# Attention and feed-forward kernel on one core: the small operations that split a unit's maxima are placed one by one between the maxima, ScalarE rounds the projections' high part, and the jobs of the step table move

## The chip, the cores and the metric

The kernel runs on one core of one Trainium2 chip. The metric is the device time of one execution in microseconds (us). The engines are named as the profile names them: PE (TensorE, with PEld for its weight loads), DVE (VectorE), ACT (ScalarE), POOL (GpSimd) and SP (SyncE, which only issues DMAs here).

## The reference, cut to what matters

```
x = x + ga * attention(layernorm(x) * (1 + ca) + sa)      # 8 batches x 1024 tokens x 256, 16 heads of 16
x = x + gb * feed_forward(layernorm(x) * (1 + cb) + sb)   # two layers of windowed attention and a gated MLP

attention(h):
    inner, outer, v = h @ Wi, h @ Wo, h @ Wv              # per head: 1024 x 16
    p    = softmax(inner @ outer.T / 4)                   # over 1024 keys
    attn = p * aperture[q] * expression[k]
    attn = attn / (attn.sum(keys) + 1e-8)
    out  = (fixed per-head rotation and scale of attn @ v) @ Wout
```

The change touches the attention alone. Its softmax needs the maximum of every query's row of logits. The feed-forward part is the same code before and after.

## The kernel before, in words

**Two stages.** The attention works through eight batches, 64 steps each, and then the feed-forward part starts. Batch 0 and batch 7 are written out straight; batches 1 to 6 are one loop body.

**Units and steps.** A batch has eight units (`u`): a group of four heads times one half of the queries. A unit has eight steps, one for each 128 keys. In step `e` PE computes transposed logits for step `e+1` in two pairs of heads (`st`, line 655), ACT takes their exponentials (`exp`, line 938, two of 128x1024), and PE multiplies those of step `e` with the values (`pv`, line 667).

**Maxima.** The exponent of a query needs its row's maximum beforehand. So for each unit PE also computes the logits the other way round, 32 blocks of 128 queries by 512 keys (`score`, line 637), and DVE reduces each to a column of maxima (`maximum`, line 1153). Four scores and four maxima go with each step, and they run `AHEAD` = 48 blocks ahead of the unit that uses them. When a unit's 32nd maximum is there, DVE combines the halves and splits the result into three bf16 parts with five operations of 128x16 (`split`, lines 1161 to 1169), each waiting for the one before. PE transposes the parts (`maxima`, line 644), DVE copies them to `mrow` (`rows`, line 1174), and SP moves the rows by three small DMAs (line 436) into `stack`, where the `st` of that unit's first step (step 7 modulo 8 of the unit before it) reads them as an extra term. With 48 blocks ahead the split falls behind the last maximum of steps 3, 11, 19, ... (3 modulo 8), and the transposition and the copy fall into steps 4, 12, 20, ...

**Banks.** Banks 5 to 7 of PSUM form a ring. The scores and the jobs below take the next bank in the order of the list `ring`: in a step with a job that is score, job, score, score, score. A tenant waits on PE until the reader of the tenant three places before it is done (`bank_free`, `taken`). So in a step with a job the last score waits for the job's reader.

**Jobs.** The table `between` gives a step at most one job: `heads` (PE transposes a unit's result, DVE normalises it, steps 2 modulo 8), `maxima` (above), `cvT` and `out` (output projection of the previous batch; DVE adds the residual), and for the next batch `hT` (transposes of the normalised input), `proj` (eight blocks 128x512 of the two f32 projections, two f32 matmuls each, line 619) and `v`.

**The projections' split.** A projection block becomes three bf16 parts. DVE copies it to bf16 (line 1129, the high part, into one of four slots of `parts`), subtracts that from the block (line 1131, into `rest`), and POOL makes the middle and low parts (lines 1572 and 1575). SP writes the four slots out (line 408) and later reads them as stacks (line 427). A slot's high part may be written only when the slot's last write-out has landed (`s_parts_out`). In a `proj` step PE runs the first matmul of the block behind the first score and the second behind the third; DVE runs the copy and the subtraction behind its third maximum.

**Order on the engines.** Each engine's order is written out by hand, in the `batch` function of each block: PE (`early`, `late`), ACT, DVE, POOL, SP.

## Time and profile before

| | us |
|---|---|
| three runs | 5584.57, 5597.72, 5596.64 |
| median | 5596.64 |
| the profiled execution | 5589.1 |
| its span, first to last instruction | 5587.3 |
| PE busy in the span | 5159.0 (92%) |
| DVE busy | 4149.6 (74%) |
| ACT busy | 2768.1 (50%) |
| POOL busy | 1136.2 (20%) |

The span is what the trace shows; the time of the profiled execution is 1.8 us more, and the median of the runs is 7.5 us above that execution. Busy time is the union of an engine's instructions. "Idle" in a row is the time the engine stood still just before it, and behind the arrow stands what released it. The granted clock (PEclk) is 1.00 at 2.4 GHz and 0.50 at 1.2 GHz. Times inside the span count from its start. Batch 4, the fourth pass of the loop body, runs from 1165.2 us (the first maximum of its step 0) to 1421.1 us (the same of batch 5); most rows are from it, and where a step is timed it goes from its first maximum to that of the next step.

### The profile page before, as it was taken

Reading aid. Unit: us, or ns where it says so; the run is one execution under the profiler, and the core shown is the slowest. Engines: PE = TensorE matmul, PEld = TensorE weight load, DVE = VectorE, ACT = ScalarE, POOL = GpSimd, SP = SyncE. Lnnn points to the kernel's source line nnn. Section 1 sums busy time; section 2 is a strip of 40 time slices with the busy share of each in tenths; the row PEclk is TensorE's granted clock in tenths of the full one; section 3 lists DMA queues with packets and bytes.
Section 4 is the critical chain, followed back from the end, with each engine's and each line's share of the span. In section 5 each row is a group of like instructions: output and inputs, shape, how many; then the busy total and the mean of one; then the engine's idle time right before and its main releaser. Section 6 shows DMA issues by size and latency. Waiting matters only on the chain.

```text
span 5587.3 us, 93191 instructions
## 1 busy us (share of the span) xinstructions
PE 5159.0 (92%) x29772; PEld 3087.8 (55%) x29772; DVE 4149.6 (74%) x10975; ACT 2768.1 (50%) x5457; POOL 1136.2 (20%) x1469
## 2 busy tenths in 40 slices
PE   4899898999989997999999999999999999999998
PEld 1233333333333334777776777777767777777776
DVE  4787777787777784777777777776777777777776
ACT  0555555555555564444444444444444544445444
POOL 2202021111112001222222222222222222222221
PEclk7999999999999999999999999999999999999999
DMA  4422233322233221000000000000000000000000
GB/s 108 105 48 56 40 62 45 63 50 46 51 54 61 39 39 33 11 7 7 9 8 28 7 11 7 6 11 28 7 11 6 7 9 26 11 9 8 7 8 6
DMA packets 165077, 160.91 MB, mean 29 GB/s; under 512 B 26228, under 2 KB 157128, under 8 KB 164560
## 3 DMA queue, kind: packets, MB, share of 16 engines
q1 hardware_dynamic: 164688, 156.42, 13.2%
q8 instruction: 159, 2.61, 0.2%
q14 instruction: 230, 1.88, 0.1%
HBM read 111.48 MB, written 44.09 MB: 28 GB/s over the span
## 4 chain that ended last, share of the span: by engine, by line
PE 73%; DVE 16%; issue 6%; SPq 1%; POOL 1%; DMA 1%; ACT 0%; DVEq 0%; POOLq 0%; ACTq 0%
PE psum L875 13%; PE psum L807 9%; PE psum L637 8%; PE psum L667 7%; PE psum L655 6%; PE psum L782 6%; DVE mx L1153 5%; PE psum L846 4%; PE psum L855 4%; PE psum L838 4%; PE psum L830 3%; PE psum L819 2%; DVE big_s L1349 2%; DVE big_s L1364 1%; PE psum L627 1%
## 5 line engine op out<-in xcount | busy, mean ns | idle before, releaser
L1153 DVE TENSOR_REDUCE mx<-psum 128x1 f32<-128x512 f32 x2048 | 1322.6, 687 | 405.8 <-PE psum L637 395.6
L938 ACT ACTIVATE pr<-psum 128x1024 f32<-128x1024 f32 x1024 | 1021.2, 1023 | 868.4 <-PE psum L655 860.4
L637 PE MATMUL psum<-stack 96*128 96x512 bf16 x2048 | 748.7, 396 | 170.2 <-DVE mx L1153 101.9
L995 ACT ACTIVATE big_s<-big_s,mxl_s 128x256 f32<-128x256 f32 x1024 | 507.5, 496 | 654.3 <-DVE mxl_s L1357 654.3
L875 PE MATMUL psum<-hlT_s,w_sb 128*128 128x128 f32 (+1 forms) x6144 | 786.5, 281 | 24.3 <-DVE hlT_s L1394 22.0
L875 PEld LDWEIGHTS psum<-hlT_s,w_sb 128*128 128x128 f32 (+1 forms) x6144 | 692.5, 179 | 158.0 <-ACT hlT_s L1010 55.3
L807 PE MATMUL psum<-wqkv_sb,uT_s 128*128 128x512 f32 x1536 | 747.8, 610 | 1.0 <-DVE uT_s L1310 1.0
L637 PEld LDWEIGHTS psum<-stack 96*128 96x128 bf16 x2048 | 199.4, 97 | 886.3 <-DVE mx L1153 381.7
L655 PE MATMUL psum<-stack 99*128 99x512 bf16 x2048 | 627.9, 389 | 31.4 <-issue 25.7
L667 PE MATMUL psum<-pr,vg 128*32 128x512 f32 x4096 | 564.6, 624 | 0.4 <-ACT pr L938 0.4
L830 PE MATMUL psum<-kT_s,qz_s 128*128 128x256 f32 x2048 | 516.8, 391 | 0.0
L1349 DVE CUSTOM_DVE_ANT_0 big_s<-psum,mask_s,rn_s 128x256 f32<-128x256 f32 x1024 | 437.5, 478 | 12.0 <-PE psum L830 5.4
L830 PEld LDWEIGHTS psum<-kT_s,qz_s 128*128 128x128 f32 x2048 | 367.1, 192 | 112.6 <-ACT qz_s L987 52.2
L1623 POOL TENSOR_TENSOR rn_s<-ss_s,neghalf 128x8 f32<-128x8 f32 x256 | 420.2, 1656 | 19.3 <-POOL ss_s L1619 0.5
L977 ACT ACTIVATE pT_s<-psum 128x1024 f32<-128x1024 f32 x128 | 131.1, 1024 | 566.8 <-PE psum L807 565.3
L782 PE MATMUL psum<-w_sb,pT_s 128*128 128x256 f32 (+1 forms) x1536 | 393.4, 398 | 6.9 <-issue 5.1
L807 PEld LDWEIGHTS psum<-wqkv_sb,uT_s 128*128 128x128 f32 x1536 | 264.7, 192 | 230.0 <-issue 198.3
L782 PEld LDWEIGHTS psum<-w_sb,pT_s 128*128 128x128 f32 (+1 forms) x1536 | 272.8, 190 | 102.3 <-issue 60.0
L1364 DVE TENSOR_SCALAR big_s<-big_s,rz_s 128x256 f32<-128x256 f32 x1024 | 315.7, 351 | 18.2
L655 PEld LDWEIGHTS psum<-stack 99*128 99x128 bf16 x2048 | 202.4, 100 | 214.8 <-issue 75.1
L1405 DVE SCALAR_TENSOR_TENSOR pT_s<-psum,b_sb,pT_s 128x128 f32<-128x128 f32 (+1 forms) x768 | 209.0, 343 | 122.7 <-ACT pT_s L1018 115.2
L1018 ACT ACTIVATE pT_s<-psum,b_sb 128x128 f32<-128x128 f32 (+1 forms) x768 | 216.5, 367 | 167.2 <-PE psum L875 166.4
(165 smaller groups left out, 6565.1 us busy)
## 6 DMA issues: line engine op xcount, KB each, us to landing
stack<-parts_d SPq DMA_DIRECT2D x384, 128.0 KB, 5.8
parts_d<-parts SPq DMA_DIRECT2D x64, 384.0 KB, 2.6
hn<-in_x SPq DMA_DIRECT2D x8, 1024.0 KB, 8.1
xr<-in_x SPq DMA_DIRECT2D x8, 1024.0 KB, 5.5
x_d<-xr SPq DMA_DIRECT2D x8, 1024.0 KB, 8.7
tab<-tab_d SPq DMA_DIRECT2D x32, 256.0 KB, 2.6
mask_s<-in_mask SPq DMA_DIRECT2D x64, 128.0 KB, 2.2
out_x<-o_s SPq DMA_DIRECT2D x64, 128.0 KB, 1.7
```

Source lines behind the costliest of these rows:

```text
L637: pe.matmul(psum[:, to, :], stack[0:KS, g % 2, 0, u % 2, h, a * P:(a + 1) * P], stack[0:KS, g % 2, 1, kh, h, :], start=True, stop=True).th ...
L655: mm = pe.matmul(psum[:, h, :], stack[0:KS + PART, (u // 2) % 2, 1, kc // 4, h, (kc % 4) * P:(kc % 4 + 1) * P], stack[0:KS + PART, (u // 2 ...
L667: mm = pe.matmul(psum[h * VW:(h + 1) * VW, ACC, :], vg[:, (u // 2) % 2, kc, h, :], pr[:, e % 2, h, :], start=(kc == 0), stop=(kc == NT - 1))
L782: mm = pe.matmul(psum[:, bk, 0:D], hid[0:rows, cc, :], w2_sb[0:rows, l, cc, :], start=(cc == 0), stop=(cc == FC - 1))
L807: mm = pe.matmul(psum[:, bk + m, :], w["uT"][:, l, k * (P + 1):k * (P + 1) + P], wqkv_sb[:, l, k, m * INNER:(m + 1) * INNER], start=(k == ...
L830: mm = pe.matmul(psum[:, bk + h // 2, (h % 2) * 2 * P:(h % 2 + 1) * 2 * P], w["qz"][:, h, :], w["kT"][:, l, h // 2, :], start=True, stop=True)
L875: mm = pe.matmul(psum[0:rows, bk + 1 + m // 4, (m % 4) * P:(m % 4 + 1) * P], w1_sb[:, l, k, col:col + rows], w["hlT"][:, k, :], start=(k = ...
L938: act.activation(pr[:, e % 2, 2 * pair:2 * pair + 2, :], psum[:, 2 * pair:2 * pair + 2, :], ACT.Exp, scale=DH ** -0.5).then_inc(s_exp, 1)
L995: ins = act.activation(w["big"][:, h, :], w["big"][:, h, :], ACT.Exp, bias=w["mx"][:, h:h + 1], accum_out=w["z"][:, h:h + 1])
L1153: dve.tensor_reduce(mx[:, u % 2, m, kh:kh + 1], psum[:, src, :], AX.X, ALU.max).then_inc(s_max, 1)
L1349: ins = dve.tensor_tensor_reduce(out=w["big"][:, h, :], in0=psum[:, bk + h // 2, (h % 2) * 2 * P:(h % 2 + 1) * 2 * P], in1=w["mask"][:], s ...
L1623: gp.tensor_tensor(w["rn"][:, half_h], w["ss"][:, half_h], neghalf[:, 0:LH], ALU.pow).then_inc(w["s_rn"], 1)
```

## The change

1. The five operations of `split` are taken apart. The first stands behind the second maximum of the following unit, and the other four behind the next four maxima, one each.
2. `AHEAD` goes from 48 to 51. A unit's last maximum is now the first of step 3 modulo 8; the five operations stand in steps 3 and 4 modulo 8 (two, then three), and the `maxima` job moves from steps 4 to steps 5 modulo 8, in PE's order from behind the third score to behind the first, in DVE's (`rows`) from behind the third maximum to behind the second.
3. ACT writes a projection block's high part (`high_part`), between the two exponentials of the step; it waits for PE and for the slot. DVE waits for ACT (`s_hi`) and only subtracts, now behind its second maximum.
4. Both matmuls of a projection block run together behind the first score.
5. The jobs are placed anew around the `maxima` steps.

```
-AHEAD = MU + 16
+AHEAD = MU + 19
...
-            between[NT * u + 4] = ("maxima", u + 1)
-        for kind, places in (("cvT", (5, 6, 7, 8)), ("out", (9, 11, 13, 15)), ("hT", (23, 24, 25, 27)),
-                             ("proj", (29, 31, 33, 35, 37, 39, 41, 43)), ("v", (38, 40, 45, 46, 47, 48, 49, 51))):
+            between[NT * u + 5] = ("maxima", u + 1)
+        for kind, places in (("cvT", (4, 6, 7, 8)), ("out", (9, 11, 12, 14)), ("hT", (22, 23, 24, 25)),
+                             ("proj", (28, 30, 31, 33, 35, 36, 38, 40)), ("v", (39, 41, 43, 44, 46, 47, 48, 49))):
...
+            def high_part(b, n, src):
+
+                act.wait_ge(s_proj, b * BLOCKS + (n + 1))
+                act.wait_ge(s_parts_out[n % 4], FREE + b * 32 + 16 * (n // 4))
+                act.activation(parts[:, n % 4, 0], psum[:, src, :], ACT.Copy).then_inc(s_hi, 1)
...
             def split_block(b, n, src, prev):
 
-                c0, ps = b * (2 * BLOCKS), psum[:, src, :]
-                dve.wait_ge(s_proj, b * BLOCKS + (n + 1))
-                dve.wait_ge(s_parts_out[n % 4], FREE + b * 32 + 16 * (n // 4))
+                dve.wait_ge(s_hi, b * BLOCKS + (n + 1))
                 if prev or n >= 2:
-                    dve.wait_ge(s_part, c0 + (2 * n - 2))
-                dve.tensor_copy(parts[:, n % 4, 0], ps).then_inc(s_rest, 1)
-                dve.wait_ge(s_rest, c0 + (2 * n + 1))
-                dve.tensor_tensor(rest[:, n % 2], ps, parts[:, n % 4, 0], ALU.subtract).then_inc(s_rest, 1)
+                    dve.wait_ge(s_part, b * (2 * BLOCKS) + (2 * n - 2))
+                dve.tensor_tensor(rest[:, n % 2], psum[:, src, :], parts[:, n % 4, 0], ALU.subtract).then_inc(s_rest, 1)
...
                 def next_maximum(q):
                     if not absent("score", q, first, last):
                         maximum(b, q, bank(place["score", q]))
+                    u, step = (q - MU) // MU, (q - MU) % MU - 1
+                    if 0 <= step < 5 and not absent("maxima", u, first, last):
+                        split(b, u, step)
...
                     next_maximum(q0 + 1)
+                    if kind == "proj":
+                        split_block(b + 1, n, src, True)
+                    elif kind == "maxima":
+                        rows(b, n, src)
                     next_maximum(q0 + 2)
-                    if kind == "maxima":
-                        rows(b, n, src)
-                    elif kind == "proj":
-                        split_block(b + 1, n, src, True)
-                    elif kind == "out":
+                    if kind == "out":
                         residual(b, n, src)
                     elif kind == "v":
                         logits(b + 1, n, src)
                     next_maximum(q0 + 3)
-                    if (q0 + 3) % MU == MU - 1 and not absent("score", q0 + 3, first, last):
-                        split(b, (q0 + 3) // MU)
```

**What moves on DVE around a unit's split.** The place is in batch 0, steps 18 to 20; the first row starts behind the normalisation of step 18, `m` and `mr` are the split, `mrow` the copied rows. Before:

```order
L1153 TENSOR_REDUCE mx<-psum 128x1 x7
L1161 TENSOR_TENSOR m<-mx 128x16
L1163 CAST m<-m 128x16
L1165 TENSOR_TENSOR mr<-m 128x16
L1167 CAST m<-mr 128x16
L1169 TENSOR_TENSOR m<-mr,m 128x16
L1153 TENSOR_REDUCE mx<-psum 128x1 x3
L1174 COPY mrow<-psum 48x128
```

The same place of the changed kernel, steps 18 to 21:

```order
L1158 TENSOR_REDUCE mx<-psum 128x1 x6
L1167 TENSOR_TENSOR m<-mx 128x16
L1158 TENSOR_REDUCE mx<-psum 128x1
L1170 CAST m<-m 128x16
L1158 TENSOR_REDUCE mx<-psum 128x1
L1173 TENSOR_TENSOR mr<-m 128x16
L1158 TENSOR_REDUCE mx<-psum 128x1
L1176 CAST m<-mr 128x16
L1158 TENSOR_REDUCE mx<-psum 128x1
L1179 TENSOR_TENSOR m<-mr,m 128x16
L1158 TENSOR_REDUCE mx<-psum 128x1 x3
L1184 COPY mrow<-psum 48x128
```

The count of operations is the same; one reduction stands between any two of the five, and the rows' copy comes a step later.

**What moves on PE in a projection step.** The place is in batch 0, the first block of batch 1 (`hT,wi_sb`) with the scores (`stack`, line 637), the transposed logits (line 655) and the product with the values (`pr,vg`). Before:

```order
L637 MATMUL psum<-stack 128x512
L619 MATMUL psum<-hT,wi_sb 128x512
L655 MATMUL psum<-stack 128x512 x2
L637 MATMUL psum<-stack 128x512 x2
L619 MATMUL psum<-hT,wi_sb 128x512
L667 MATMUL psum<-pr,vg 32x512 x4
L637 MATMUL psum<-stack 128x512
```

and of the changed kernel:

```order
L638 MATMUL psum<-stack 128x512
L621 MATMUL psum<-hT,wi_sb 128x512 x2
L656 MATMUL psum<-stack 128x512 x2
L638 MATMUL psum<-stack 128x512 x2
L668 MATMUL psum<-pr,vg 32x512 x4
L638 MATMUL psum<-stack 128x512
```

The second matmul of the block has moved ahead of the transposed logits and of two scores.

## Rows read from the trace of the kernel before

**Rows 1.** The page: busy time by engine.
```profile
PE 5159.0 (92%) x29772; PEld 3087.8 (55%) x29772; DVE 4149.6 (74%) x10975; ACT 2768.1 (50%) x5457; POOL 1136.2 (20%) x1469
```

**Rows 2.** Windows: batches 0, 4 and 7; stretch, length, busy times, PEclk, DMA.
```profile
147.40:392.50 245.10, 219.09 (x1141) 73.25 (x1140) 195.56 (x376) 136.53 (x150) 40.43 (x36) 0.98 0.31 68
1165.20:1421.10 255.90, 230.76 (x1193) 83.47 (x1192) 199.22 (x383) 138.99 (x153) 40.79 (x37) 0.96 0.28 52
1929.10:2103.40 174.30, 164.40 (x912) 55.80 (x911) 147.12 (x277) 107.27 (x114) 4.08 (x7) 1.00 0.24 38
```

**Rows 3.** Windows: batch 4, steps 32; 18 to 21; 51 to 53; 9 to 15.
```profile
1284.11:1286.95 2.84, 2.84 (x17) 1.04 (x16) 2.60 (x5) 1.86 (x3) 2.11 (x3) 1.00 1.14 128
1233.88:1247.14 13.26, 12.12 (x70) 3.84 (x69) 11.94 (x27) 7.84 (x9) 0.00 (x0) 1.00 0.58 165
1373.41:1384.90 11.49, 9.73 (x54) 3.19 (x53) 8.88 (x20) 6.45 (x9) 0.00 (x0) 1.00 0.02 3
1199.01:1228.20 29.19, 27.41 (x148) 11.77 (x146) 23.79 (x53) 14.16 (x16) 19.74 (x12) 1.00 0.20 29
```

**Rows 4.** Windows: batch 4, steps 31; 40; 43; 36 and 37; 44 and 45.
```profile
1278.85:1284.11 5.26, 4.62 (x21) 1.49 (x20) 3.92 (x7) 2.72 (x4) 0.85 (x2) 1.00 1.15 143
1323.20:1327.35 4.15, 3.88 (x21) 1.67 (x20) 2.73 (x6) 2.35 (x4) 0.92 (x1) 1.00 0.27 95
1336.21:1343.01 6.80, 5.08 (x23) 1.59 (x21) 5.44 (x12) 3.42 (x4) 1.76 (x2) 1.00 0.00 2
1302.45:1313.80 11.35, 9.91 (x35) 3.26 (x36) 6.77 (x12) 2.29 (x4) 0.85 (x2) 0.71 0.11 37
1343.01:1353.39 10.38, 9.36 (x35) 3.57 (x36) 5.53 (x12) 2.67 (x5) 0.00 (x0) 0.67 0.11 39
```

**Rows 5.** Timeline, steps 18 to 21: start, length, engine, line, operation, [idle before <- releaser].
```profile
1235.52 4.51 DVE L1153 TENSOR_REDUCE mx<-psum 128x1 f32<-128x512 f32 x7
...
1240.06 0.17 DVE L1161 TENSOR_TENSOR m<-mx 128x16 f32<-128x16 f32 x1
...
1241.00 1.89 DVE L1153 TENSOR_REDUCE mx<-psum 128x1 f32<-128x512 f32 x3
1241.74 0.39 PE L637 MATMUL psum<-stack 96*128 96x512 bf16 x1 [1.14 <-DVE mx L1153]
...
1242.80 0.21 DVE L1174 COPY mrow<-psum 48x128 bf16<-48x128 bf16 x1
1243.09 1.84 SPq L436 DMA_DIRECT2D stack<-mrow  x3
```

**Rows 6.** Timeline, batch 5, step 3: a small operation that waits for none before it.
```profile
1437.20 0.17 DVE L1169 TENSOR_TENSOR m<-mr,m 128x16 bf16<-128x16 f32 x1
1437.29 0.22 DVE L1148 TENSOR_SCALAR za<-zt 128x128 f32<-128x128 f32 x1
```

**Rows 7.** Timeline, step 31: a projection step on PE, DVE and ACT.
```profile
1280.37 1.29 DVE L1153 TENSOR_REDUCE mx<-psum 128x1 f32<-128x512 f32 x2 [0.82 <-PE psum L637]
1280.38 1.02 PE L619 MATMUL psum<-hT,wi_sb 128*128 128x512 f32 x2
...
1281.57 0.68 DVE L1129 CAST parts<-psum 128x512 bf16<-128x512 f32 x1
1282.29 0.69 DVE L1131 TENSOR_TENSOR rest<-psum,parts 128x512 f32<-128x512 f32 x1
1282.55 0.60 ACT L932 ACTIVATE o_sb<-psum 128x512 f32<-128x512 f32 x1 [1.38 <-PE psum L667]
...
1283.04 0.39 PE L637 MATMUL psum<-stack 96*128 96x512 bf16 x1 [0.64 <-DVE rest L1131]
...
1283.46 2.60 DVE L1153 TENSOR_REDUCE mx<-psum 128x1 f32<-128x512 f32 x4 [0.48 <-PE psum L637]
```

**Rows 8.** Timeline, the queue of SP: the first write-outs of slots in batch 4.
```profile
1291.33 10.77 SPq L408 DMA_DIRECT2D parts_d<-parts  x4
```

**Rows 9.** Landing of the rows' DMAs (line 436) in batch 4.
```profile
DMA to landing us min/median/max: 1.6/1.8/2.7
```

65 lines of the change are left out of this document (37 added, 28 removed).

## The prediction

> **What bounds the kernel now.** I read the page's busy times first: PE is busy 92% of the span, DVE 74%, ACT 50% [rows 1]. That is a mean over two stages, and only the attention is touched, so the windows come next, batch by batch and then step by step. Batch 4 takes 255.9 us and PE is idle in 25.1 of them, with a mean granted clock of 0.96 [rows 2]. A step without a job takes 2.84 us, with PE busy for all of it and DVE for 2.60 [rows 3]. So a plain step is bound by PE, with DVE only 0.24 behind, and anything on DVE beyond that shows up as PE waiting for a bank of the ring. Two places do so. The timeline of steps 18 to 21 shows the split: PE's only idle time in 13.26 us is 1.14 us, in front of a score that waits for the maximum behind the five small operations [rows 3, 5]. The projection steps take 5.26 us with PE busy for 4.62, and end in a score that waits 0.64 us for DVE's subtraction [rows 4, 7]. Where both meet the step takes 6.80 us, and the 10.38 us right behind it (steps 44 and 45) run at a granted clock of 0.67, the 11.35 us of steps 36 and 37 at 0.71 [rows 4], which is a mix of the levels 2.4 and 1.2 GHz after PE has stood still.
>
> **The change, part by part.** I cost it for a full batch, in batch 4's rows.
>
> *Split, in a unit with light steps.* DVE runs seven reductions back to back from 1235.52 to 1240.06, 0.65 us each from start to start although each is listed with 0.69, then the five operations up to 1241.00, 0.94 us, each waiting for the one before [rows 5]. In the new order two of the five stand before that reduction, apart from each other, and need not wait. What such an operation costs DVE no row shows for the split itself. The nearest is the `za` operation, which starts 0.09 us after a small operation it doesn't depend on [rows 6]; the other end is the whole 0.17 us, or 0.94/5 = 0.19. I take 0.09, since the reductions' 0.65 against 0.69 shows the same overlap. The reduction at 1241.00 then starts at 1240.24, and the score at 1241.74 is 0.76 us earlier. Some 0.1 of it is lost again: the other three operations and the row copy add 0.4 us to DVE where it has 0.24 a step to spare. Gain 0.65 us; the ends are 0.3 (at 0.19 each) and 1.14 (no idle time left). The step with the transposition gives back nothing more, since PE and DVE do the same work there as before.
>
> Here the Trainium skill speaks against the change. VectorE: DVE Perf Modes, section "The DRAIN you can't avoid", says that the next operation doesn't start until the pipeline has emptied, with or without semaphores between, and advises to cut the number of operations, which this change leaves as it is. The trace disagrees in part: 0.09 from start to start for an operation 0.17 long [rows 6]. By that rule the gain would be the lower end, some 22 us less in the whole.
>
> *Split, beside jobs.* What the split and the transposition cost now above the bare steps: steps 43 and 44, 6.80 - 5.26 = 1.54 and about 0.47 for the transposition's step, together 2.0, and the same for 35 and 36; steps 51 to 53, 11.49 against 4.15 + 2 x 2.84, is 1.66 [rows 3, 4]; for the units of steps 11 and 27 I take the 1.3 of the light unit (13.26 against 3.44 for a step with heads and 3 x 2.84; 3.44 is my reading of step 18). In the new table the steps beside jobs (11 and 12, 28, 35 and 36, 43 and 44) have DVE idle before the second maximum, so only what stands between the second maximum and the job's reader counts: 0.1 to 0.2 a step and 0.2 for the transposition, 0.5 a unit. Saved: three light units 2.0, unit 11 0.7, unit 27 0.8, units 35 and 43 3.0, unit 51 (light from now on) 1.0. **7.5 us.** Steps 9 to 15, 29.19 us now [rows 3], should take 28.4.
>
> *Projection steps.* Now the last score stands 2.66 us behind the start of the second matmul: 1.19 to the copy, 0.72 to the subtraction, 0.69 for it, 0.06 to PE [rows 7]. In the new order the second matmul starts 0.87 earlier, as four bf16 matmuls of some 0.22 no longer stand before it (my estimate: a step of 2.84 has eight of them beside the values' product). From there PE needs 0.9 for the matmul and 0.65 up to the second score, whose reduction starts 0.42 behind it [rows 7]; that reduction ends 2.4 behind the matmul's start. ACT has the high part by 1.19 + 0.60 = 1.8 (priced like its other 128x512 copy [rows 7]), so DVE doesn't wait for ACT; the subtraction ends at 3.05 and the score follows at 3.05. The step gains 0.87 + 2.66 - 3.05 = 0.48. PE's own work sets the floor at 4.6, a gain of 0.65; if ACT's copy came late the gain could go to nothing. ACT's copy itself is hidden: ACT is busy for 2.72 of 5.26 us [rows 4]. Its cover would be gone only if the second exponential came later than the next step's product, some 2 us on. Eight steps: **3.9 us.**
>
> *Clock.* Steps 36 and 37 take 11.35 against about 3.3 + 5.26, steps 44 and 45 10.38 against 3.3 + 4.15 [rows 4]: 2.8 and 2.9 us, both right behind a step of 6.80. With those steps at about 5 us and PE's idle time there cut to some 0.3, I expect the clock to stay at 2.4 GHz. **5.7 us.** The ends are nothing and this. Batch 0 shows 0.98 where batch 4 shows 0.96 [rows 2], so I give it none.
>
> *Waits that move.* ACT now waits for the slot of block 4, with the exponentials queued behind it. The write-outs start at 1291.33, 12.5 us behind the start of step 31 [rows 4, 8]. Blocks 4 to 7 are needed from step 35 on, 4.8 + 2.8 + 4.8 + 3.4 = 15.8 us behind the start of step 31, and the trigger in step 30 comes 1.9 earlier relative to it, as that step grows; so the slot should be free with over 2 us left. The rows of maxima go out 2.6 us later (from 1.8 us behind the start of step 20 to 4.4), while step 23 comes 0.65 earlier. They leave at 1243.09 in three issues of 0.6 us and land 1.8 us later [rows 5, 9], at 1246.1, and are needed at about 1249.6, so 3.5 us of cover shrink to 0.2. That is nothing at the median landing and 0.7 at the longest, 2.7 [rows 9], in the units with light steps behind.
>
> *Start and end.* Three more scores stand before batch 0 (1.9 us), three fewer in batch 7 (0.8 back). **1 us lost.** The first projection blocks are paced by POOL's two operations and the DMAs; nothing.
>
> *Sum.* Full batch: 7.5 + 3.9 + 5.7 = 17.1, six times 103. Batch 0 has 11.4. Batch 7 has no jobs for a next batch, seven units at 0.65: 4.5. 103 + 11 + 4.5 - 1 = 117 or 118. From the profiled execution's 5589.1 that gives 5472. The median of the runs stands 7.5 above that execution, so I put the median at **5475 us**, 2.2% less.
>
> **The rivals.**
> *A, small operations don't overlap.* Each costs DVE 0.19 wherever it stands. For it: the 0.94 for five. Against: 0.09 for `za` [rows 5, 6]. About 0.35 less a unit over 62 units is 22 us: 5497.
> *B, the clock falls all the same*, behind other idle times (the projection steps keep some). For it: it falls twice in batch 4 for reasons of which I know only that idle time went before. Against: step 31 has 0.64 idle and shows 1.00 [rows 4, 7]. 5.7 x 6 = 34 us: 5509.
> *C, slower: the maxima's rows land too late.* The first `st` of each unit waits for three DMAs, and PE's whole queue stands behind it. It has 0.2 us left. The 62 units save 1.9 each, so it decides from a landing of some 3.9 us instead of 1.8. If the rows came behind a large load and took 6 us, each unit would wait 4.0, 248 us against 117: 5605 to 5610. Against it: 2.7 was the longest of 24 [rows 9].
> *D, no change*: C in part, or ACT waiting for slots, eats what is gained: 5590.
>
> **How the numbers follow.** The forecast has 0.64, A 0.14, B 0.13, D 0.04, C 0.05. The forecast's own range runs from all idle time of the units gone (62 x 0.5 = 30 us) and the projections at PE's floor (9 us), 5436, to the lower ends of both, about 5495. With A and B the range is **5436 to 5515**, which leaves out C and D and little else. A measurement of this kernel can tell some 0.3%, 17 us, from no change. Faster by more than that: forecast, A, B, and a little of D, 0.92; within 0.3% 0.04; slower 0.04.
>
> **What would show it.** In the changed profile: steps 18 to 21 in about 12.6 us with 0.5 us of PE idle; a small operation between two reductions moving the next one by about 0.1; projection steps at 4.8 us, the score behind the subtraction waiting some 0.2; steps 35 to 37 and 43 to 45 at a clock of 1.00, full batches at 0.98 and near 239 us. It is wrong if steps 7 modulo 8 begin with PE waiting for the rows' DMAs, if ACT is idle before a high part in steps 35 to 40, or if low-clock stretches appear inside a batch.

## The result, and the profile after

The changed kernel takes 5416.08 us (median of 4 runs, 5414.40 to 5417.96), the kernel before 5590.60 (5583.30 to 5597.72) beside it: a ratio of 0.9688, with an interval of 0.9671 to 0.9705. That is 3.1% less. The prediction said 5475 and a range of 5436 to 5515: the sign was right, and the gain, 175 us of span (5587.3 to 5412.5), is half as much again as the 118 forecast. The time lies 20 us below the lower end of the range.

The busy line of the page, changed kernel, which answers to [rows 1]:
```profile
PE 5115.0 (95%) x29772; PEld 3075.7 (57%) x29772; DVE 4064.5 (75%) x10911; ACT 2800.6 (52%) x5521; POOL 1135.6 (21%) x1469
```
DVE has 64 instructions less and ACT 64 more, the high parts. PE's instructions are as many as before; of what went, 131 us are its idle time (428 us before and 298 now) and 44 us its busy time, which is shorter where the clock is no longer low.

Windows of the changed kernel: batches 0 and 4, which answer to [rows 2]; batch 7 up to the feed-forward stage; the feed-forward stage.
```profile
147.92:377.23 229.31, 217.21 (x1141) 72.50 (x1140) 184.94 (x368) 140.53 (x158) 40.36 (x36) 0.98 0.33 70
1081.03:1316.19 235.16, 225.58 (x1193) 81.71 (x1192) 188.43 (x376) 143.17 (x162) 40.76 (x37) 0.99 0.31 57
1779.04:2023.10 244.06, 211.79 (x1134) 75.92 (x1133) 159.58 (x314) 134.80 (x146) 16.15 (x24) 0.94 0.21 45
2023.10:5412.50 3389.40, 3269.78 (x20197) 2413.95 (x20195) 2527.33 (x7852) 1649.47 (x4221) 797.09 (x1144) 1.00 0.03 10
```
The last two of these in the kernel before:
```profile
1929.10:2179.70 250.60, 211.11 (x1136) 75.83 (x1135) 163.98 (x316) 134.50 (x146) 16.09 (x24) 0.95 0.22 44
2179.70:5587.30 3407.60, 3275.25 (x20198) 2414.13 (x20196) 2527.89 (x7852) 1649.05 (x4221) 797.45 (x1144) 0.99 0.03 10
```
Batch 4 takes 20.7 us less, batch 0 15.8, batch 7 6.5 between these borders. The fourth window is the surprise: the feed-forward stage, whose code the change doesn't touch, is 18.2 us shorter.

Windows inside batch 4 of the changed kernel: steps 18 to 21; 51 to 53; 9 to 15; 31; 36 and 37; 44 and 45 ([rows 3, 4] before).
```profile
1146.73:1159.02 12.29, 12.26 (x71) 3.88 (x70) 11.59 (x27) 7.85 (x9) 0.00 (x0) 1.00 0.76 192
1272.83:1281.49 8.66, 8.66 (x50) 2.48 (x48) 8.17 (x20) 5.96 (x8) 0.00 (x0) 1.00 0.01 2
1113.26:1141.05 27.79, 27.43 (x147) 11.75 (x146) 23.14 (x53) 14.15 (x16) 18.36 (x12) 1.00 0.18 25
1191.19:1195.99 4.80, 4.63 (x21) 1.49 (x20) 3.12 (x7) 3.21 (x5) 1.99 (x3) 1.00 1.08 147
1212.66:1219.97 7.31, 7.05 (x36) 2.17 (x35) 6.16 (x15) 3.62 (x6) 1.82 (x3) 1.00 0.01 3
1245.39:1252.81 7.42, 6.99 (x38) 2.54 (x37) 5.72 (x16) 4.34 (x6) 0.00 (x0) 1.00 0.01 2
```
Read the first number behind the stretch, its length, against the second, PE's busy time: in the light steps PE is now busy for all but 0.03 us. Steps 18 to 21 take 12.29 in batch 4 but 12.09 or 12.10 in four of the six batches of the loop, where the kernel before takes 13.27 in each. Steps 51 to 53 held a `v` job in the kernel before and hold none now, so their two rows are not of the same work. The projection step is at 4.80, as forecast, and the two places behind the old 6.80 us steps run at a clock of 1.00.

Timeline of DVE in steps 19 and 20 of batch 4, changed kernel, which answers to [rows 5]:
```profile
1152.39 0.69 DVE L1158 TENSOR_REDUCE mx<-psum 128x1 f32<-128x512 f32 x1 [0.16 <-PE psum L638]
1153.00 0.16 DVE L1170 CAST m<-m 128x16 bf16<-128x16 f32 x1
1153.07 0.68 DVE L1158 TENSOR_REDUCE mx<-psum 128x1 f32<-128x512 f32 x1
1153.67 0.16 DVE L1173 TENSOR_TENSOR mr<-m 128x16 f32<-128x16 f32 x1
1153.76 0.68 DVE L1158 TENSOR_REDUCE mx<-psum 128x1 f32<-128x512 f32 x1
```
From one reduction's start to the next it is 0.68 or 0.69 us with a small operation between them, 0.65 without [rows 5]. So a single operation listed with 0.16 costs 0.03 to 0.04 there.

**Where the 174.8 us went**, with batch starts taken at the first reduction of step 0: the feed-forward stage 18.2; batch 0 15.8; batches 1 to 6 134.7 (1536.6 to 1401.9), batch 7 6.6, less 0.5 for the start. Of the 134.7, 13.7 lie at the five places where the loop over the batches goes back (steps 63, 0 and 1: 16.9 to 21.2 us each before, 14.9 to 16.9 now; e6_before_pad217 below has the attention's code of the kernel before and its five edges took 6.0 less than those of the kernel before, so the 13.7 is good to some 6 us); the other 121 are 20.2 a batch, where 17.1 were forecast.

### The profile page after: what moved, and what is told of

Same layout as the page of the kernel before. It is cut to its first block, busy times and chain, and to the rows that moved or that the text cites. A ratio compares the mean times of both kernels' runs of the same rounds, so it can differ in the third digit from the quotient of the medians.

```text
span 5412.5 us, 93107 instructions
## 1 busy us (share of the span) xinstructions
PE 5115.0 (95%) x29772; PEld 3075.7 (57%) x29772; DVE 4064.5 (75%) x10911; ACT 2800.6 (52%) x5521; POOL 1135.6 (21%) x1469
## 4 chain that ended last, share of the span: by engine, by line
PE 77%; DVE 12%; issue 5%; SPq 2%; DMA 2%; POOL 1%; ACT 0%; DVEq 0%; POOLq 0%; ACTq 0%
PE psum L874 14%; PE psum L806 10%; PE psum L638 8%; PE psum L656 7%; PE psum L668 7%; PE psum L781 7%; PE psum L845 5%; PE psum L854 4%; PE psum L829 4%; PE psum L837 4%; DVE mx L1158 3%; PE psum L818 2%; PE psum L621 2%; DVE big_s L1361 2%; DVE big_s L1376 1%
## 5 line engine op out<-in xcount | busy, mean ns | idle before, releaser
L638 PE MATMUL psum<-stack 96*128 96x512 bf16 x2048 | 732.3, 391 | 56.4 <-DVE zt L1142 16.8
L668 PE MATMUL psum<-pr,vg 128*32 128x512 f32 x4096 | 550.3, 610 | 0.4 <-ACT pr L943 0.4
L1376 DVE TENSOR_SCALAR big_s<-big_s,rz_s 128x256 f32<-128x256 f32 x1024 | 315.5, 350 | 18.2
```

The lines of the kernel that those rows point to most:

```text
L638: pe.matmul(psum[:, to, :], stack[0:KS, g % 2, 0, u % 2, h, a * P:(a + 1) * P], stack[0:KS, g % 2, 1, kh, h, :], start=True, stop=True).th ...
L668: mm = pe.matmul(psum[h * VW:(h + 1) * VW, ACC, :], vg[:, (u // 2) % 2, kc, h, :], pr[:, e % 2, h, :], start=(kc == 0), stop=(kc == NT - 1))
```

## The experiments

The theory to be tested first is the prediction's: the gain within a batch is the split's idle time, the second matmul with ACT's copy, and the low clock. Rivals are named in the expectations. Each ran timed beside the kernel before. Batch lengths below are sums over the 64 steps of the median in batches 1 to 6: 256.7 us before, 234.4 changed.

**The two parts alone.** e1_split_only is the changed kernel with the projection as before:
```
-    act.activation(parts[:, n % 4, 0], psum[:, src, :], ACT.Copy)     # high_part
+    dve.tensor_copy(parts[:, n % 4, 0], ps)                           # split_block, behind the third maximum
     second matmul back in late()
```


> The changed kernel with the projections as they were before: DVE makes the high part and subtracts, both behind its third maximum, and PE runs a block's second matmul behind the third score. AHEAD, the table and the five separate operations stay as changed. Theory 1 (the split is most of the gain, the projections about 0.48 us for each of 8 blocks in 7 batches): 27 us over the changed kernel's 5416, so 5443 us, with light units still at 12.3 us, projection steps at 5.26, and no low clock inside a batch. Theory 2 (the projections' new form is what keeps PE going and the clock up): low clock back in steps 35 to 45 and 5480 us or more. Either may be off by some 18 us if the feed-forward loops come out in another state.

e2_proj_only is the kernel before with the changed projection, and the old tables, AHEAD and split.

> The kernel before with the projections alone in their new form: both matmuls behind the first score, ACT makes the high part, DVE subtracts behind its second maximum. AHEAD 48, the five chained operations and the old table stay. Theory 1: 8 x 0.48 us in 7 batches, 27 us off 5590, so 5563 us; the light units stay at 13.3 us, and since steps 35 and 43 still hold the split the clock still falls behind them. Theory 2: the falls of the clock go with the projections' waits, another 34 us, 5530 us.

Measured: 5477.47 us (0.9808, interval 0.9788 to 0.9827) and 5523.65 (0.9887, 0.9868 to 0.9906). Neither hit its number: e1 is 34 us above its 5443 and e2 6 below even its second theory. The reason lies outside the work of the two parts. The feed-forward stage is 3406.4 in e1 and 3393.8 in e2, and the five edges of the batch loop sum to 96.3 us in e1 and 79.2 in e2, against 93.8 before and 80.1 changed: both go with the projection part, which shortens DVE's code. Take them off, and e1 is 28 us above the changed kernel, where theory 1 had 27.

A batch takes 241.5 and 249.1, so 15.2 and 7.6 less than before, 22.8 together, near the 22.3 that both bring. That holds the edges. Inside the batches (means of steps 2 to 62) it is 239.1 before, 218.9 changed, 222.5 in e1 and 232.9 in e2: 16.6 and 6.2 less, 22.8 against 20.2. So the parts add up but for 2.6 us a batch. Each may remove a share of the same low clock; that isn't shown. The low clock is gone inside e1's batches although its projection steps still take 5.26, and stays in e2, whose steps 35 and 43 take 6.33.

**Are the small operations better apart?** e3_grouped:
```
-    if 0 <= step < 5 and not absent("maxima", u, first, last):
-        split(b, u, step)
+    if step == 0 and not absent("maxima", u, first, last):
+        for k in range(5): split(b, u, k)
```


> The changed kernel with one edit: the five small operations stand together again, chained, behind the second maximum of the next unit, where the first of them stands in the changed kernel. Theory 1 (what counts is that a maximum stands between any two): the chain costs DVE 0.94 us at once instead of some 0.3 in five places, PE idles about 0.7 us again in each of 62 units, so 5416 + 43 = 5459 us, light units at 13.0 to 13.3. Theory 2 (what counts is the new place, three blocks further ahead and away from the jobs, and the transposition a step later): under 10 us more, 5425.

e8_maxima_late puts the transposition behind the third score and the row copy behind the third maximum; e16_grouped_late does both; e9_ahead48 is e8 with `AHEAD = MU + 16`.

> The changed kernel, with the maxima's transposition back behind the third score of its step and the row copy back behind the third maximum (before the change they stood there too; the step stays the fifth of the unit, the five small operations stay apart, the projection as in the change). The kernel with the five operations together in the new place lost only 25 us of what the split part brings (85), so the place must bring most. Theory R (what counts is that transposition and row copy stand early in their step, beside the second score): per unit 0.5 to 0.8 us back, 62 units, 5450 to 5466, with a light unit (steps 18 to 21) at 12.9. Rival S (what counts is that the transposition comes a step later, so that PE has a full ring of scores ahead of it): within 8 us of the changed kernel, 5416 to 5424, light unit 12.3 to 12.4.

> The kernel with the late transposition (5429.9), and beside it AHEAD back at MU + 16: three scores fewer stand ahead. A unit's last maximum is then the fourth of its fourth step again, as before the change, and the five small operations follow behind the second to fourth maximum of the fifth step and the first two... of the sixth, apart from each other; the jobs stay at the changed steps. Theory S2 (what brings most of the split part's gain is that the chain of small operations begins just ahead of PE's values' product, which needs no bank, and the transposition comes with more scores ahead): per unit 0.3 to 0.7 us more than the late transposition, 5450 to 5475. Rival R2 (the gain is in having the operations apart and the transposition a step later, wherever the last maximum stands): 5425 to 5435.

> The changed kernel with both: the five small operations together behind the maximum after a unit's last one, and the transposition and row copy late in their step. Of the unit's three steps 19 to 21 the changed kernel takes 8.66 us, with the operations together 9.00, with the late transposition 8.83, the kernel before 9.83. If the two add up, 9.2 and 5416 + 25 + 14 = 5455; what is left to the kernel before, 0.65 a unit, is then the place of the last maximum and of the group in the step alone. If they don't (one stall covers the other), 9.0 and 5441.

Measured: e3 5441.25 (0.9740, 0.9721 to 0.9759), e8 5429.88 (0.9726, 0.9709 to 0.9744), e16 5451.57 (0.9770, 0.9753 to 0.9786), e9 5477.50 (0.9802, 0.9782 to 0.9823). Steps 59 to 61 of batch 4 have no job beside the split's; one window of each, in the order before, changed, e3, e8, e16, e9:
```profile
1400.03:1409.86 9.83, 8.69 (x50) 2.56 (x48) 8.62 (x20) 5.65 (x7) 0.00 (x0) 1.00 0.01 3
```
```profile
1296.61:1305.27 8.66, 8.66 (x50) 2.48 (x48) 8.17 (x20) 5.66 (x7) 0.00 (x0) 1.00 0.01 2
```
```profile
1312.99:1322.00 9.01, 8.84 (x50) 2.48 (x48) 8.47 (x20) 5.66 (x7) 0.00 (x0) 1.00 0.01 2
```
```profile
1305.62:1314.44 8.82, 8.69 (x50) 2.56 (x48) 8.13 (x19) 5.65 (x7) 0.00 (x0) 1.00 0.01 2
```
```profile
1313.75:1322.92 9.17, 8.86 (x50) 2.56 (x48) 8.43 (x19) 5.65 (x7) 0.00 (x0) 1.00 0.01 2
```
```profile
1332.04:1341.40 9.36, 8.74 (x50) 2.56 (x48) 8.14 (x20) 5.65 (x7) 0.00 (x0) 1.00 0.01 2
```
e3 leaves only 25 us to the operations' being apart, between its theories (5459 and 5425). The unit's gain of 1.17 us comes apart: keeping the operations together costs 0.35, the late transposition 0.16, both 0.51, so they add up. The other 0.66 is left to the place: the last maximum of a unit is now the first of its step and not the fourth. It isn't the transposition's coming a step later: its step takes 3.31 in e16 as in the kernel before. What differs is the step of the operations and one plain step, 3.68 + 2.84 before against 3.32 + 2.54 in e16. The timelines show what the place does. Before, the block of five begins at 1240.06, 1.1 us behind the end of PE's values' product, with the next product still to come; PE, three banks ahead at most, runs dry [rows 5]:
```profile
1237.91 1.07 PE L667 MATMUL psum<-pr,vg 128*32 128x512 f32 x8
```
In e3 the same block begins at 1167.38, just behind a product, where DVE has caught up:
```profile
1166.19 1.06 PE L668 MATMUL psum<-pr,vg 128*32 128x512 f32 x8
...
1169.05 0.39 PE L638 MATMUL psum<-stack 96*128 96x512 bf16 x1 [0.17 <-DVE mx L1158]
```
```profile
1167.38 0.16 DVE L1167 TENSOR_TENSOR m<-mx 128x16 f32<-128x16 f32 x1
...
1168.30 3.84 DVE L1158 TENSOR_REDUCE mx<-psum 128x1 f32<-128x512 f32 x6
```
It holds DVE as long as before (0.92 us), and the waiting score loses 0.17 in place of 1.14. e9 points the same way (0.54 more than e8; 5477.50 lies just above its 5475), but there the chain also ends later, which makes its transposition's step 3.81 where 3.31 stand in e8, so it isn't a clean measure of the place. e8 fits neither of its two theories: 0.16 a unit lies between 0 and 0.5, nearer to rival S. e16 is near its 5455.

**What a small operation costs.** e11_ten_small puts one more behind each of the five:
```
+    dve.tensor_copy(idle[:, 16 * step:16 * step + 16], ident[:, 0:16])
```


> The changed kernel, with one more small operation behind each of the five (a copy of 128x16, depending on nothing). It measures what a small operation costs VectorE where PE sets the pace. My reading of the trace of after (0.65 us from one reduction to the next, 0.68 with a small operation between): 0.07 to 0.1 each, 62 units of 5: 20 to 30 us if VectorE were the bound and 0 to 15 where it isn't; 5416 to 5432, and a light unit (steps 18 to 21) at 12.3 to 12.5. Rival A (each operation empties the pipeline, 0.19 or more each): 5 x 0.19 = 0.95 a unit against the spare time of 0.24 a step, 0.5 a unit longer, 5445 or more. The 39 places of code in the feed-forward stage may change too: its own length is read apart (3389 or 3407).

Measured: 5425.96 (0.9710, 0.9690 to 0.9730), and steps 59 to 61:
```profile
1300.55:1309.34 8.79, 8.79 (x50) 2.48 (x48) 8.40 (x24) 5.66 (x7) 0.00 (x0) 1.00 0.01 3
```
The unit pays 0.13 us for five. That isn't what they cost DVE, which has time to spare there. DVE's timeline in step 20 of batch 4 has that:
```profile
1156.40 0.68 DVE L1159 TENSOR_REDUCE mx<-psum 128x1 f32<-128x512 f32 x1
1157.00 0.17 DVE L1174 TENSOR_TENSOR mr<-m 128x16 f32<-128x16 f32 x1
1157.08 0.17 DVE L1222 COPY idle<-ident 128x16 f32<-128x16 f32 x1
1157.16 0.69 DVE L1159 TENSOR_REDUCE mx<-psum 128x1 f32<-128x512 f32 x1
```
From reduction to reduction it is 0.76 us with two small operations, 0.68 with one, 0.65 with none: the first costs 0.03, the second 0.08, as the expectation had it. Rival A of the prediction (0.19 each) has fallen: the unit would have to be 0.5 longer. Some 7 us of the time are not the unit's: the feed-forward stage is 3396 us, from another place of the code (below).

**What ACT brings.** e10_dve_high is the changed kernel, with DVE making the high part directly ahead of the subtraction; both matmuls stay early. e18_dve_high_front20 is the same with a filler in the set-up, explained below.
```
-    dve.wait_ge(s_hi, b * BLOCKS + (n + 1))
+    dve.tensor_copy(parts[:, n % 4, 0], ps).then_inc(s_rest, 1)
```


> The changed kernel, but VectorE makes the projection's high part again (copy, then subtraction, both behind the second maximum), with both matmuls in one piece early in the step as in the change. Theory A (ACT's taking the copy over is what brings the projection part's gain): VectorE has 0.69 us more in each of 8 steps of a batch, of which it has no spare time in those steps, so 8 x 0.65 = 5.2 us a full batch over the changed kernel's, more where it stands beside a split and the clock falls again; with the longer code before the feed-forward loops (39 instructions) that stage goes back to 3407: 5416 + 36 + 18 = 5470, up to 5490 with the clock. Rival E (the early second matmul brings it): 5435 to 5445.

> The kernel in which VectorE makes the high part (5493), with 20 such copies in the set-up: the attention loop starts 17 behind a block's start in place of 3 before it. Theory F: the second wait for code at the 5 loop edges goes, 97 us for the 5 in place of some 81 to 83: 14 to 16 us less, 5478; the feed-forward stage at 3407 as it was. What then lies between it and the changed kernel, 62 us, is 18 of the feed-forward stage and 44 of ACT's taking the copy (8 x 0.72 us in each of 7 batches is 40). Rival H (the edge is longer because VectorE itself is more loaded there): 5493.

Measured: 5493.22 (0.9831, 0.9812 to 0.9850) and 5476.26 (0.9793, 0.9778 to 0.9808). Step 31 of batch 4, e10:
```profile
1231.48:1237.00 5.52, 4.62 (x21) 1.49 (x20) 3.80 (x8) 2.72 (x4) 2.67 (x4) 1.00 1.15 129
```
5.52 against 4.80: ACT's part is 0.72 a step, a whole copy, 8 x 7 x 0.72 = 40 us. And 5.52 is longer than the 5.26 of the kernel before [rows 4] and of e1, from which e10 differs in two things: the second matmul is early, and DVE's copy and subtraction stand behind its second maximum. Together they cost 0.26 without ACT. So the early matmul is worth nothing by itself here. ACT's copy with the matmul left late was not run. e10 as a whole is 3 us above the 5490 that was its upper end; the 17.0 us that e18 takes less say what was missed, the edges of the batch loop.

**Does a stand-still of PE bring the low clock?** e15_stall:
```
+    if e in (35, 43) and not last:
+        for k in range(4): dve.tensor_reduce(idle[:, k:k + 1], wfold, AX.X, ALU.max)
```


> The changed kernel, with four reductions of 128x512 from SBUF added on VectorE behind the third maximum of steps 35 and 43 in all but the last batch (some 2.5 us each time, which PE must wait for as the ring has three banks). Theory C (a stand-still of PE there brings the low clock, which costs a few us more than itself): low-clock stretches inside the batch, in steps 36 and 44, some 2.5 us + 2 to 3 us each time, 14 places, 5416 + 63 to 77 = 5480 to 5493. Rival N (the low clock came of something else): each place costs 2.0 to 2.5 us and no low clock appears: 5444 to 5451.

Measured: 5450.11 (0.9770, 0.9754 to 0.9786). Steps 35 and 36 of batches 2 and 3 in e15:
```profile
744.07:755.26 11.19, 9.39 (x42) 3.16 (x41) 9.65 (x20) 5.07 (x7) 2.78 (x4) 1.00 0.16 56
982.68:995.31 12.63, 10.83 (x41) 3.14 (x39) 9.82 (x20) 5.08 (x7) 3.53 (x4) 0.86 0.12 41
```
The changed kernel takes 9.67 there. PE idles 1.80 us in both windows; in one the clock stays, in the other it falls, and that costs 1.44 more. It fell in 3 of the 14 places, all behind step 35 and none behind step 43. In time the rival is right (5450 in its 5444 to 5451), and theory C missed by 30 us or more; but three falls where the changed kernel has none say that a stand-still can bring one.

The added stand-still isn't the old one. PE's longest pause in one piece is 1.83 us at the end of steps 35 and 43 of the kernel before, with one of 0.64 ahead of it: the clock fell behind 11 of these 12 steps in batches 1 to 6. In e2 it is 1.83 with 0.17 ahead: 9 of 12. In e15 it is 1.63 in step 35 (3 of 7) and 1.56 in step 43 (none of 7), and in steps 11 and 51 of the kernel before some 1.5 (5 of 12). In e1's step 35 it is 0.72 and in the changed kernel 0.17 and 0.35: never. So longer pauses went with more falls, but the same pause in the same step gave both, and what decides was not found.

**The feed-forward stage.** The window loop of this stage exists twice in the code. Counted in DVE's compiled code, the change leaves 39 instructions less ahead of both copies, which begin at 1902 and 2885 in place of 1941 and 2924. e4_nops39 was to put 39 back as empty instructions; none of them was emitted, so it is a repeat of the changed kernel, and tells only how well that repeats.

> The changed kernel with 39 empty instructions on DVE between the attention and the feed-forward part, where DVE idles for 15 us on a DMA. They move DVE's later code by about as many instructions as the kernel before had more. Theory P (the feed-forward stage differs by 18 us between the two kernels only by where the code of DVE's two copies of the window loop lies, since the branch back takes 2.8 us in one state and 0.3 in the other): the first copy slow and the second fast again, about 18 us more, 5434 us, the attention unchanged. Rival (the feed-forward stage differs for another reason, as its start relative to the clock or to the DMAs): within 3 us of 5416.

It took 5418.18 (0.9697, 0.9678 to 0.9716). Real ones followed, copies of one column, where DVE waits for a DMA ahead of the stage (e5, e6, e7), or between the two copies (e12):
```
+    for j in range(39): dve.tensor_copy(idle[:, j:j + 1], ident[:, 0:1])     # e5; 217 in e6, 20 in e7, 40 in e12
```


> The changed kernel with 39 copies of one column more on VectorE, between the attention's last residual and the feed-forward stage, where VectorE waits some 15 us for a DMA. They move the two copies of VectorE's feed-forward window loop 39 instructions further, to the very places they have in the kernel before (loop starts at instructions 1941 and 2924 of VectorE's code in place of 1902 and 2885); the attention's code stays where it is. Theory P (the feed-forward stage became 18 us shorter only because shorter code before it put the loops at other places): VectorE's step back to the start of the loop takes 2.8 us in the first copy and 0.3 in the second, as before, the stage takes 3407 us in place of 3389, the whole 5434. Rival Q (the stage is shorter for another reason, such as the state in which the attention leaves the clock or the queues): 3389 and 5416 to 5420.

> The kernel before with 217 such copies at the same place: its loops start at 2158 and 3141, which is 256 instructions behind where the changed kernel has them. Theory P, with places that count modulo 256: first copy fast (0.3 us back), second slow (2.8), feed-forward stage 3389 to 3394, the whole 5572 to 5576, against 5588 of the kernel before; the 217 copies take some 13 us of VectorE, most of it in its 15 us of waiting. Rival Q: 3407 and 5588 or more. If places count over a longer period than 256 the state may be another one.

> The changed kernel with 20 such copies: loops start at 1922 and 2905, 130 and 89 modulo 256. Fast places so far are 108 and 110, slow ones 69 and 149. If the fast places form one stretch that reaches from 89 to 130, both copies are fast: 5 iterations of the second copy save 1.4 us each, stage 3382 to 3385, the whole 5409. If the stretch is narrow, both are slow: stage 3414, the whole 5441. One of each gives 3389 or 3407.

> The changed kernel with 40 copies of one column on VectorE between the first and the second copy of its feed-forward window loop (once in the run, 2 to 3 us of VectorE). The first copy stays at 1902 (110 modulo 256, fast), the second moves from 2885 to 2925 (69 to 109 modulo 256, where the fast ones have stood). Theory P: both copies fast, 5 x 1.4 = 7 us saved, less the 2 to 3 that the copies take: feed-forward stage 3384 to 3386, the whole 5411 to 5413. Rival Q2 (the second copy is slow for another reason than its place): 3392 and 5419.

Measured: e5 5435.81 (0.9741, 0.9725 to 0.9757), its stage 3410.0; e6 5570.28 (0.9979, 0.9969 to 0.9989), 3397.6; e7 5423.98 (0.9719, 0.9703 to 0.9736), 3396.3; e12 5413.31 (0.9684, 0.9664 to 0.9703), 3387.1. The timeline of DVE where the first copy of the loop steps back, kernel before:
```profile
2470.76 0.17 DVE L1357 TENSOR_SCALAR mxl_s<-mxl_s 128x4 f32<-128x4 f32 x1
2473.89 0.42 DVE L1285 TENSOR_TENSOR u_s<-psum,u_s 128x256 f32<-128x256 f32 x1 [2.96 <-issue]
...
2579.80 0.42 DVE L1285 TENSOR_TENSOR u_s<-psum,u_s 128x256 f32<-128x256 f32 x1 [2.93 <-issue]
```
Changed kernel:
```profile
2313.49 0.17 DVE L1369 TENSOR_SCALAR mxl_s<-mxl_s 128x4 f32<-128x4 f32 x1
2314.98 0.42 DVE L1297 TENSOR_TENSOR u_s<-psum,u_s 128x256 f32<-128x256 f32 x1 [1.33 <-PE psum L781]
...
2419.53 0.42 DVE L1297 TENSOR_TENSOR u_s<-psum,u_s 128x256 f32<-128x256 f32 x1 [1.32 <-PE psum L781]
```
And e5, the changed kernel with its code moved back to the old places:
```profile
2532.76 0.42 DVE L1300 TENSOR_TENSOR u_s<-psum,u_s 128x256 f32<-128x256 f32 x1 [2.96 <-issue]
```
Before, DVE waits 2.96 us at the step back for nothing that the profile shows; now it waits 1.33 for PE, as the loop's work wants. An iteration takes 105.9 in the one case and 104.55 in the other. Before, the first copy (15 steps back in all) pays and the second (5) doesn't; in the changed kernel it is the other way round: (15 - 5) x 1.36 = 14 us, and the rest of the 18 is the scatter of this stage, 3389 to 3397 in kernels with one code layout. e5 brings the wait and the 18 to 20 us back with nothing else changed, which settles it. e6 does the reverse in the kernel before, 256 places further than the changed kernel's loops, with a stage 10 us shorter. Both of e12's copies are free, and its 5413.31 is what was expected. e7's second copy, at 89 modulo 256, paid 2.8 us, against the first expectation; its first, at 130, was free.

**The loop over the batches.** It steps back across more code than any other, and each time DVE and ACT stand still for about 6 us (from the branch to the next instruction 4.8 to 6.8 us on DVE and 4.6 to 6.7 on ACT in the 20 traces). Some kernels show a second wait right behind. e13_before_front20 and e14_front30 have 20 and 30 of the one-column copies in the set-up, ahead of all loops, e17_front34 34.

> The kernel before with 20 copies of one column on VectorE in the set-up, where it waits 20 us. They move VectorE's attention loop from instruction 600 to 620 of its code (88 to 108 modulo 256), its feed-forward loops from 1941 and 2924 to 1961 and 2944. Theory F (after the step back VectorE comes to a second block of code some 5 to 8 instructions behind the loop's start, at about 96 modulo 256, and waits 3 to 5 us for it once more; in the changed kernel, which starts at 586, 22 instructions lie before it and it has come by then): with the start behind that point the second wait is gone, steps 63 to 1 of a loop edge take 15 to 17 us in place of 17 to 21, 6 edges 12 to 18 us in all, and the low clock there is shorter. The feed-forward copies: 169 modulo 256 slow as before, 128 fast as before, 3407. The whole 5570 to 5576 against 5588. Rival H (the edges are shorter because the changed jobs leave another backlog): 5588.

> The changed kernel with 30 such copies in the set-up, 29 instructions more in all: attention loop from 586 to 615 (103 modulo 256), feed-forward loops to 1931 and 2914 (139 and 98 modulo 256). If fast places are those from about 96 to 146 modulo 256, both feed-forward copies are fast, which saves 7 us and costs nothing elsewhere: stage 3382 to 3388. The attention's edges as they are, 15 to 17 us, or 0.5 us shorter each. The whole 5406 to 5411: the candidate that beats the changed kernel. If 98 lies before the boundary the second copy stays slow, 5416; if 139 is too late the first is slow, 5434.

> The changed kernel with 34 copies of one column on VectorE in the set-up (33 instructions more), where it waits 20 us. Its attention loop then starts at 13 of a block, its feed-forward loops at 46 and 2. Theory P: both copies at 104.6 us an iteration, no wait of 2.8 us at their steps back: stage 3382 to 3385, the whole 5408 to 5411, 0.13% less than the changed kernel. If 46 is too far (52 is slow) the first copy costs 15 x 1.4: 5430; if 2 is too near the start, the second copy costs 1.4 or 4.5 each time: 5416 or 5434.

Timeline of DVE behind the step back into a batch, kernel before:
```profile
1165.21 0.69 DVE L1153 TENSOR_REDUCE mx<-psum 128x1 f32<-128x512 f32 x1 [5.55 <-PE psum L637]
1166.49 0.69 DVE L1153 TENSOR_REDUCE mx<-psum 128x1 f32<-128x512 f32 x1 [0.59 <-PE psum L637]
1169.97 4.43 DVE L1153 TENSOR_REDUCE mx<-psum 128x1 f32<-128x512 f32 x7 [2.79 <-PE psum L637]
```
e10:
```profile
1116.83 0.69 DVE L1158 TENSOR_REDUCE mx<-psum 128x1 f32<-128x512 f32 x1 [5.88 <-PE psum L638]
1122.45 3.68 DVE L1158 TENSOR_REDUCE mx<-psum 128x1 f32<-128x512 f32 x6 [4.93 <-issue]
```
e18, the same kernel 20 instructions on:
```profile
1348.97 0.69 DVE L1159 TENSOR_REDUCE mx<-psum 128x1 f32<-128x512 f32 x1 [5.39 <-PE psum L639]
1350.25 1.29 DVE L1159 TENSOR_REDUCE mx<-psum 128x1 f32<-128x512 f32 x2 [0.59 <-PE psum L639]
1352.74 2.59 DVE L1159 TENSOR_REDUCE mx<-psum 128x1 f32<-128x512 f32 x4 [1.21 <-PE psum L639]
```
In e10 DVE does one reduction and waits 4.93 us once more; in the kernel before it does two, and the seven reductions that then run in one piece (1169.97) show that PE had the scores ready long before, so the 2.79 put down to PE are not PE's. In the compiled code both stand at the same instruction, 606, at which they stop: their loops begin at 603 and 600. The changed kernel's begins at 586, and by the time DVE gets there nothing is waited for. e18 takes 17.0 us less than e10; e13 took 5569.54 beside 5579.23 (0.9979, 0.9970 to 0.9989), its five edges 15.9 to 16.8 us in place of 16.9 to 21.2, 12 us in all.

e14 took 5434.47 (0.9737, 0.9721 to 0.9754), a miss: the second copy, at 98 modulo 256, pays twice. Its step back:
```profile
4859.73 0.42 DVE L1300 TENSOR_TENSOR u_s<-psum,u_s 128x256 f32<-128x256 f32 x1 [5.13 <-issue]
```
There DVE stops at the loop's start (2.8 us) and again two instructions on, at instruction 2916. Leaving out the labels, which are no instructions, 606 and 2916 are 576 and 2880: 2304 apart, 9 x 256. So both stops are at the starts of blocks of 256 instructions. Counted from a block's start (one more than in the later expectations, which had it one too far), the window loop of 333 instructions began, over all 20 kernels, at 3, 9, 10, 14, 29, 30, 34, 43, 47 and 129 where the step back took 0.3 us, and at 53, 73, 85, 226, 242, 246 and 255 where it took 2.8 or more. The Trainium skill, Runtime: NRT & Kernel Launch, section "Instruction fetch mechanics", says that an engine holds two pages of 256 instructions and that a step back to a page it no longer holds must fetch it first. The traces agree in kind, with 2.8 us for the window loop and about 6 for the batch loop. A loop of 333 that starts anywhere up to 179 lies in two pages and would by that rule be free. The runs disagree: 53, 73 and 85 weren't. 47 + 333 is 380 and 53 + 333 is 386, which looks as if the loop had to end within its first one and a half blocks; but the start at 129 ends at 462 and was free. It is the first copy in e11, beside its second, at 85:
```profile
2321.91 0.42 DVE L1299 TENSOR_TENSOR u_s<-psum,u_s 128x256 f32<-128x256 f32 x1 [1.32 <-PE psum L782]
...
4862.22 0.42 DVE L1299 TENSOR_TENSOR u_s<-psum,u_s 128x256 f32<-128x256 f32 x1 [3.02 <-issue]
```
What fits all 17 starts is a count in half blocks of 128: the loop was free where it touches three of them (instructions 0 to 383 for the starts at 3 to 47, 128 to 511 for 129) and paid where it touches four. That was read off these starts afterwards, and no run was made to test it.

e17 took 5413.54 (0.9681, 0.9668 to 0.9694). Both its copies step back in 0.3 us and each iteration takes 104.6, as designed, but its stage is 3388.9 long, not 3382 to 3385: the turns of the outer loop and the end are 1 to 3 us longer, and with ranges of 5407.8 to 5417.6 and 5414.4 to 5418.0 neither e17 nor e12 can be told from the changed kernel. Nothing tried beats it by more than it scatters.

## Why the prediction was right and wrong

It was right in the sign and in the size of the projection's term, and the low clock went as forecast; it was too small by 57 us. Two steps failed. The split's term was mis-sized: it gave a light unit 0.65 us, from shortening the chain of five, and the unit gained 1.17, of which 0.35 come of the operations' being apart, 0.16 of the early transposition and 0.66 of where in the step the unit ends, which the prediction didn't price. And it put the place of the code at nothing, on the ground that "only the attention is touched": 31.9 us, 18.2 of them in the feed-forward stage. With these 31.9 us the time would have been 5448, inside the range. By its own steps:

- *Light unit, "I take 0.09 ... Gain 0.65 us".* Measured 1.17, just above the upper end of its bounds (1.14). A single operation between two reductions costs 0.03, not 0.09. The 0.1 of other work on DVE was charged for nothing, since PE's idle time there has gone to 0.03. And most of the gain is of another kind than the step had: it let the reductions start earlier behind a shorter block, while 0.66 of 1.17 comes of where in the step a unit ends. The term missed about 0.5 in each light unit, and with it most of the 25 us that the batches' insides gained beyond the forecast.
- *The Trainium skill against the change.* The prediction took half of what is said there. The same section of the Trainium skill, "The DRAIN you can't avoid" in VectorE: DVE Perf Modes, adds that a next operation that is not held (made to wait until every earlier one has finished) starts earlier, and the advice to keep the number of operations small stands in another section, "Rules for kernel authors". The traces agree with the addition: 0.68 us from one reduction to the next over a small operation, where the reduction alone is listed with 0.68.
- *"The step with the transposition gives back nothing more."* It does: 0.16 a unit (e8).
- *Split beside jobs, 7.5 us a batch.* Steps 9 to 15 came out at 27.79 (28.4 forecast). Steps 51 to 53 went from 11.49 to 8.66, but 1.31 of the 2.83 is the `v` job (4.15 - 2.84 [rows 3, 4]), which moved to another step; 1.52 is saved, where 1.0 was forecast, 0.5 too little again.
- *Projection steps, 0.48 each.* 5.26 to 4.80, 0.46, and 3.6 us a batch between e1 and the changed kernel (3.9 forecast): right, and so was the wait of the score behind the subtraction, forecast at some 0.2:
```profile
1194.17 0.68 DVE L1136 TENSOR_TENSOR rest<-psum,parts 128x512 f32<-128x512 f32 x1
...
1194.91 0.39 PE L638 MATMUL psum<-stack 96*128 96x512 bf16 x1 [0.17 <-DVE rest L1136]
```
- *Clock, 5.7 us a batch.* Steps 36 and 37 went from 11.35 to 7.31, 44 and 45 from 10.38 to 7.42, all at a clock of 1.00, with the jobs in them partly others. No low clock is left within batches 1 to 6. Right in kind, and in size by some luck: 11.35 was the longest of six (10.2 to 10.3 in the others), while the clock also fell in step 12 of three of these batches and step 52 of two, which batch 4 doesn't show. In all the kernel before had 10 to 14 us of low clock inside each of batches 1 to 6. That it is the stand-still that brings it was only half borne out (e15).
- *Waits that move.* Right as far as seen. ACT is idle ahead of each of the 56 high parts of batches 1 to 7, some 0.9 us, which the prediction had as a sign of being wrong in steps 35 to 40; but it waits for PE's matmul there, never for a slot. From batch 0's first step on PE waits twice for the rows' DMAs. One wait, 4.68 us at 174.76 in batch 0, is old (5.07 us at 176.37 in the kernel before); the new one is of 0.73 us, near the end of batch 7, rival C in small:
```profile
1952.51 1.04 PE L656 MATMUL psum<-stack 99*128 99x512 bf16 x4 [0.73 <-DMA stack<-mrow]
```
- *Batch 0, 11.4, and batch 7, 4.5.* 15.8 and 6.6, from the light units' term again.
- *What no step had:* the feed-forward stage, 18.2, and DVE's second wait for code at five loop edges, 13.7. "Only the attention is touched" was true of the work and not of the places of the code. The rows were there to be seen: 2.96 us of `issue` at 2473.89 of the kernel before.

The sum: 57.3 us missed = 18.2 + 13.7 + 6 x 3.07 in the batches' insides (18.4) + 4.4 in batch 0 + 2.1 in batch 7 + 0.5 at the start. Rival A has fallen (0.03 us for a small operation between two reductions, 0.08 for a second beside it), B too within this kernel, and C and D with the result. Rival C's price was added up wrongly besides: 248 us of waits against a gain of 117 is 131 above 5590, so about 5720, not 5605 to 5610. And the range's upper part left out that the projections' gain could go to nothing, as the prediction itself says: with light units at 0.3 that is 5475 + 22 + 27 = 5524, not 5495.

## What to carry to other kernels

Where an engine with little spare time has a block of extra work per unit, look first at where in the repeating step the block falls: right behind the partner's long stretch that needs nothing of this engine it cost 0.17 us, right ahead of it 1.14, for the same 0.92 us of work. Moving a copy to an engine with time to spare and moving a matmul forward were worth 0.46 a step together, and the second one without the first less than nothing. And a change of an engine's number of instructions moves every loop behind it: compare the idle time put down to `issue` at each step back, in stages that weren't touched as well, before a few tenths of a per cent are credited to an edit.

## What the runs showed of the hardware that was not expected

- A loop's step back on DVE takes 0.3 us or 2.8 to 3.1 us (branch to next instruction) by its place in the code, with identical instructions, and 5.1 in all where its start lies just ahead of a block of 256 (e14). For the loop over batches it is 4.8 to 6.8 on DVE and 4.6 to 6.7 on ACT each time, and 4.93 more for the next block in e10's row.
- A DVE operation of 128x16, listed with 0.16 us, costs 0.03 between two reductions of 128x512 from PSUM, and a second one beside it 0.08 (e11).
- With the same 1.80 us of PE idle in the same two steps, the clock stayed in one batch and fell in another (e15, 1.00 and 0.86); a fall there cost 1.44 us.
- A wait that the profile puts down to PE can be one for code: the seven reductions in one piece behind it tell.
